# A Mamba-2 block with a routed expert layer: the order of work within a period is moved on all five engines

## The chip, the cores and the metric

The kernel runs on one core of a Trainium2 chip, in one launch. Its time is the device time of that core in microseconds (us). The engines are PE (TensorE matrix products), DVE (VectorE), ACT (ScalarE), POOL (GpSimd) and SP (SyncE, which here only issues transfers). Each engine takes its own list of instructions strictly from front to back; engines wait for each other through semaphores alone.

## The reference

```
x   (16, 512, 128), f32
mod = silu(c) @ wmod                      # sa, ca, ga, sb, cb, gb per sequence
h   = layernorm(x) * (1 + ca) + sa
x   = x + ga * mamba2(h)                  # scan over 512 steps, 4 heads of 64, state 128
h   = layernorm(x) * (1 + cb) + sb
x   = x + gb * moe(h)                     # 8 experts, top 2 of them per token

mamba2: zxbcdt = h @ W_in.T; causal conv of 4 taps and silu over x, B, C
        dt = softplus(dt + dt_bias); state = state * exp(dt*A) + dt*x (outer) B; y = state . C
        y = (y + D*x) * silu(z); y * rsqrt(mean(y*y)+eps) * norm_w; y @ W_out.T
moe:    logits = h @ Wg.T; top 2, softmax of the two
        out = sum over the two experts of w * ((silu(h@W1+b1) * (h@W2+b2)) @ W3 + b3)
```

Everything is f32. The 16 sequences are independent in the Mamba part; the expert part mixes the tokens of all.

## The kernel before, in words

**Pairs.** Two sequences are one pair (8 pairs, 0 to 7). A pair passes these steps, and each is a small function of the kernel: moments1, power_norm1, shift_norm1, normalise1, turn_norm1, modulate1 (first layer norm, transposed into h); project_in 0 to 7 into the two PSUM banks T0 and T1, each followed by conv_first (ACT), conv_taps (DVE) and per channel tile conv_silu (ACT, line 604); project_z and z_silu; time_steps, softplus_exponent, softplus_exp, softplus_rest (dt); masked_da, segments and decay_exp (the decay matrices, through the banks YA and YB); attention, masked_g, mix_chunk; per chunk of 128 steps to_tokens, weight_by_dt and weight_by_decay (POOL, lines 406 and 415), intra, inter, new_state, next_state, y_chunk, turn_y, take_yt, squares; and at the end mean_square, power_y, project_out (line 1389), residual, moments2, power_norm2, shift_norm2, normalise2, turn_norm2, modulate2, logits, turn_h2, load_payload, top_two, which_two, ranks (line 1424), rows, scatter 0 to 7 (POOL, line 427: the pair's rows go to DRAM by expert) and new_tiles, which lists what tiles of one expert's rows are full.

**Tiles.** A tile is 256 rows of one expert; 71 tiles are run, 8 per pair and the last 22 after the last pair. For a tile, SP loads its weights (line 298) and rows (line 318); PE turns the rows (expert_turn, line 1434, bank FX), multiplies them up (expert_up, two halves in banks FG and FV, line 1444) and down (expert_down, lines 1451 and 1457, bank FX again); ACT does expert_input and expert_silu, DVE expert_hidden (line 1125) and expert_out (line 1133); POOL adds the result to the output in DRAM with two indirect DMAs (add_out, line 457). Rows of one token lie in two tiles, so add_out(t) waits until the one before it has landed up to tile 49, and after that only where the two tiles can hold the same token. Tiles 8p-7 to 8p belong to pair p: their rows can be loaded once all eight scatters of pair p have landed. A rows buffer is free again when the add_out seven tiles earlier has landed; a weights buffer after the expert_down four tiles earlier.

**What sets the order.** Each engine has a loop over a period i, whose body is a list of such steps for pairs i-2 to i+3 and tiles 8i-k. The list is fixed text; no scheduler moves anything. While the last steps of pair p run, the first steps of pair p+1 and eight tiles run between them. From pair 3's period on all the tiles of a period are there; before, a period has pair work alone, and after the last pair there are tiles alone.

## Time and profile before

| what | value |
|---|---|
| median of 3 runs | 832.32 us (821.59 to 838.61) |
| profiled execution, its own time | 832.36 us |
| its span | 830.5 us, 1.9 us around it |
| PE / DVE / ACT / POOL busy | 82% / 67% / 62% / 56% of the span |
| mean granted TensorE clock | 0.916 |

The span has four parts. Up to about 246 us there is pair work alone: a period is from one project_out to the next. From there to about 612 us pairs and tiles run together. From 612 us the last pair ends and its rows are scattered, beside tiles of the pair before; from about 709 us only tiles are left. The busy time is an average over these parts, so each is read on its own: from a table of windows, and from the engines' timelines in order of time.

### The profile page before, as it was taken

Reading aid. Unit: us, or ns where it says so; the run is one execution under the profiler, and the core shown is the slowest. Engines: PE = TensorE matmul, PEld = TensorE weight load, DVE = VectorE, ACT = ScalarE, POOL = GpSimd, SP = SyncE. Lnnn points to the kernel's source line nnn. Section 1 sums busy time; section 2 is a strip of 40 time slices with the busy share of each in tenths; the row PEclk is TensorE's granted clock in tenths of the full one; section 3 lists DMA queues with packets and bytes.
Section 4 is the critical chain, followed back from the end, with each engine's and each line's share of the span. In section 5 each row is a group of like instructions: output and inputs, shape, how many; then the busy total and the mean of one; then the engine's idle time right before and its main releaser. Section 6 shows DMA issues by size and latency. Waiting matters only on the chain. (4 is left out here: it accounts for less than half of the span.)

```text
span 830.5 us, 13734 instructions
## 1 busy us (share of the span) xinstructions
PE 680.6 (82%) x3713; PEld 518.9 (62%) x3713; DVE 559.4 (67%) x1640; ACT 516.8 (62%) x1223; POOL 462.0 (56%) x366
## 2 busy tenths in 40 slices
PE   3678899789789999998999999999966952774982
PEld 3246557556567776876787777768755731553662
DVE  2827967988986997898689978987743561231421
ACT  3784795896796899687969977886522310221320
POOL 2003004444453378757775786688687477357775
PEclk9779798999998999999999999999996967897997
DMA  5100001112013465455346444653645774857973
GB/s 186 28 0 1 1 27 32 45 52 71 33 58 102 119 168 129 105 155 125 92 105 174 107 97 103 204 104 90 180 107 120 200 204 95 202 123 149 191 169 28
DMA packets 81275, 88.86 MB, mean 107 GB/s; under 512 B 7360, under 2 KB 67696, under 8 KB 81200
## 3 DMA queue, kind: packets, MB, share of 16 engines
q1 hardware_dynamic: 54528, 61.37, 25.6%
q0 software_dynamic: 26672, 26.62, 18.0%
q8 instruction: 31, 0.51, 0.3%
q14 instruction: 44, 0.36, 0.2%
HBM read 54.50 MB, written 33.46 MB: 106 GB/s over the span
## 5 line engine op out<-in xcount | busy, mean ns | idle before, releaser
L457 POOL DMA_INDIRECT out<-xs x142 | 226.8, 1597 | 116.9 <-issue 53.2
L427 POOL DMA_INDIRECT rows<-payload,pos x128 | 131.6, 1028 | 68.2 <-issue 30.2
L880 DVE SCALAR_TENSOR_TENSOR xbc<-T,table,xbc 128x511 f32<-128x511 f32 (+2 forms) x192 | 141.9, 746 | 7.7 <-ACT xbc L599 3.1
L1133 DVE SCALAR_TENSOR_TENSOR xs<-FX,xs 128x128 f32<-128x128 f32 x142 | 43.1, 345 | 122.6 <-PE FX L1457 104.7
L1457 PE MATMUL FX<-wt,hid 128*128 128x128 f32 x568 | 87.8, 301 | 17.2 <-DVE hid L1125 17.2
L655 ACT ACTIVATE xt<-FX 128x256 f32<-128x256 f32 x71 | 27.0, 380 | 110.1 <-PE FX L1434 96.0
L1457 PEld LDWEIGHTS FX<-wt,hid 128*128 128x128 f32 x568 | 73.7, 203 | 26.6 <-DVE hid L1125 17.9
L648 ACT ACTIVATE sg<-FG,wt 128x256 f32<-128x256 f32 x142 | 59.3, 471 | 47.0 <-PE FG L1444 38.4
L1444 PE MATMUL FG<-xt,wt 128*128 128x256 f32 x284 | 77.6, 397 | 12.1 <-DMA wt<-in_wt 8.1
L1287 PE MATMUL T<-h,win 128*128 128x512 f32 x128 | 76.7, 698 | 12.4 <-DVE xbc L880 10.6
L1444 PE MATMUL FV<-xt,wt 128*128 128x256 f32 x284 | 78.2, 400 | 0.0
L630 ACT ACTIVATE mda<-table,da 128x128 f32<-128x128 f32 x256 | 77.7, 397 | 0.0
L1125 DVE SCALAR_TENSOR_TENSOR hid<-FV,wt,sg 128x256 f32<-128x256 f32 x142 | 62.0, 479 | 22.5 <-issue 13.3
L599 ACT ACTIVATE xbc<-T,table 128x512 f32<-128x512 f32 x64 | 49.5, 773 | 40.3 <-PE T L1287 35.8
L385 POOL TENSOR_TENSOR rstd<-var,table 128x8 f32<-128x8 f32 x16 | 26.6, 1663 | 78.4 <-DVE var L826 63.9
L1346 PEld LDWEIGHTS YA<-xdt,decay 128*128 128x128 f32 x512 | 66.9, 207 | 2.8 <-issue 1.7
L1346 PE MATMUL YA<-xdt,decay 128*128 128x64 f32 x512 | 66.6, 288 | 1.0 <-issue 1.0
L1444 PEld LDWEIGHTS FG<-xt,wt 128*128 128x128 f32 x284 | 52.4, 200 | 20.3 <-DMA wt<-in_wt 9.7
L406 POOL TENSOR_TENSOR xdt<-tok,dt 128x512 f32<-128x512 f32 x32 | 34.8, 1088 | 51.5 <-ACT tok L566 51.3
L527 ACT ACTIVATE xn<-x,shift,rstd 128x128 f32<-128x128 f32 x128 | 50.9, 484 | 17.5 <-DVE shift L844 16.4
L1444 PEld LDWEIGHTS FV<-xt,wt 128*128 128x128 f32 x284 | 52.4, 201 | 8.5 <-issue 3.8
L1434 PE MATMUL FX<-table,xs 128*128 128x128 f32 x142 | 29.3, 290 | 31.8 <-DMA xs<-rows 27.8
(207 smaller groups left out, 1343.5 us busy)
## 6 DMA issues: line engine op xcount, KB each, us to landing
wt<-in_wt SPq DMA_DIRECT2D x71, 386.0 KB
xs<-rows SPq DMA_DIRECT2D x71, 258.0 KB
x<-in_x SPq DMA_DIRECT2D x8, 512.0 KB, 4.3
out<-x SPq DMA_DIRECT2D x8, 512.0 KB
out<-xs POOLq DMA_INDIRECT x142
rows<-pad SPq DMA_DIRECT2D x8, 258.0 KB
rows<-payload,pos POOLq DMA_INDIRECT x128
gate_a<-gates SPq DMA_DIRECT2D x8, 128.0 KB, 4.3
```

The lines of the kernel that those rows point to most:

```text
L427: pool.indirect_dma_start(d["rows"], bass.IndirectOffsetOnAxis(ap=pos[:, k, n:n + 1], axis=0), payload[:, n, :], None).then_inc(scattered, 16)
L457: pool.indirect_dma_start(d["out"], bass.IndirectOffsetOnAxis(ap=xs[:, t % XSR, c, PAY - 1:PAY].bitcast(U32), axis=0), xs[:, t % XSR, c, 0 ...
L527: last = nc.scalar.activation(dst[:, j, :], src[:, j, :], ACT.Identity, bias=shift[:, j:j + 1], scale=rstd[:, j:j + 1])
L599: nc.scalar.activation(xbc[:, t, k, :], T[:, k, :], ACT.Identity, bias=conv_b[:, t:t + 1], scale=conv_w[:, t * KC + KC - 1:t * KC + KC]).t ...
L630: last = nc.scalar.activation(mda[:, c, n, :], upto, ACT.Copy, scale=da[:, c * J + n:c * J + n + 1])
L648: last = nc.scalar.activation(sg[:, t % 2, f * TR:(f + 1) * TR], FG[:, f * TR:(f + 1) * TR], ACT.Silu, bias=wt[:, t % WR, B12 + f:B12 + f ...
L880: last = nc.vector.scalar_tensor_tensor(out=xbc[:, t, k, tap:L], in0=T[:, k, 0:L - tap], scalar=w, in1=xbc[:, t, k, tap:L], op0=ALU.mult, ...
L1125: last = nc.vector.scalar_tensor_tensor(out=hid[:, t % 2, f, :], in0=FV[:, f * TR:(f + 1) * TR], scalar=wt[:, t % WR, B12 + FT + f:B12 + F ...
L1287: nc.tensor.matmul(T[:, k, :], win[:, o:o + P], h[:, k * L:(k + 1) * L], start=True, stop=True).then_inc(in_psum, 1)
L1346: last = nc.tensor.matmul(YA[:, o:o + HD], decay[:, c, k, hh, :], xdt[:, c % 2, k, hh * HD:(hh + 1) * HD], start=True, stop=True)
L1444: last = nc.tensor.matmul((FG, FV)[v][:, f * TR:(f + 1) * TR], wt[:, t % WR, w:w + P], xt[:, t % 2, :], start=True, stop=True)
L1457: last = nc.tensor.matmul(FX[:, TR + c * D:TR + (c + 1) * D], hid[:, t % 2, f, c * P:(c + 1) * P], wt[:, t % WR, DOWN + f * D:DOWN + (f + ...
```

## The change

On every engine the steps of the period are listed in another order. The operations, their sizes, buffers and semaphore waits are the same, and every engine has as many steps as before (PE 660, ACT 557, DVE 420, POOL 223, SP 165). Most of the diff is the same list begun at another step; what is really moved is a few steps against their neighbours. Of each engine the parts that matter, as the diff has them:

```diff
@@ sync
-            for i in range(-1, 13):
...
+            for i in range(1, 14):
+                if is_tile(PT * i - 40):
+                    load_rows(PT * i - 40)
+                if is_tile(PT * i - 39):
+                    load_weights(PT * i - 39)
+                if is_pair(i - 3):
+                    store_x1(i - 3)
+                if is_pair(i):
+                    reload_x(i)
+                if is_tile(PT * i - 39):
+                    load_rows(PT * i - 39)
+                if is_tile(PT * i - 38):
+                    load_rows(PT * i - 38)
+                    load_weights(PT * i - 38)
+                if is_tile(PT * i - 37):
+                    load_weights(PT * i - 37)
+                if is_tile(PT * i - 36):
+                    load_weights(PT * i - 36)
+                if is_tile(PT * i - 37):
+                    load_rows(PT * i - 37)
...
@@ gpsimd
+                if is_tile(PT * i - 27):
+                    add_out(PT * i - 27)
+                if is_pair(i - 2):
                     scatter(i - 2, 7)
+                if is_pair(i):
+                    weight_by_dt(i, 1)
+                    weight_by_decay(i, 1)
                 if is_tile(PT * i - 26):
                     add_out(PT * i - 26)
+                if is_pair(i):
+                    weight_by_dt(i, 2)
                 if is_pair(i + 2):
                     power_norm1(i + 2)
                 if is_pair(i):
-                    weight_by_dt(i, 2)
                     weight_by_decay(i, 2)
                 if is_tile(PT * i - 25):
                     add_out(PT * i - 25)
+                if is_pair(i):
+                    weight_by_dt(i, 3)
                 if is_tile(PT * i - 24):
                     add_out(PT * i - 24)
...
@@ scalar
+                    masked_da(i, 2)
+                    z_silu(i, 3)
+                if is_tile(PT * i - 27):
+                    expert_silu(PT * i - 27)
+                if is_tile(PT * i - 26):
+                    expert_input(PT * i - 26)
+                if is_pair(i + 1):
+                    modulate1(i + 1)
+                if is_pair(i):
+                    conv_silu(i, 3)
                     decay_exp(i, 0)
...
@@ vector
                 if is_pair(i + 1):
                     mix_chunk(i + 1, 1)
+                    mix_chunk(i + 1, 2)
                 if is_pair(i + 2):
                     softplus_exponent(i + 2)
-                if is_pair(i + 1):
-                    y_chunk(i + 1, 0)
-                    next_state(i + 1, 0)
-                    mix_chunk(i + 1, 2)
...
+                if is_pair(i + 2):
+                    softplus_rest(i + 2)
+                if is_tile(PT * i - 13):
+                    expert_hidden(PT * i - 13)
+                if is_tile(PT * i - 14):
+                    expert_out(PT * i - 14)
+                if is_pair(i + 2):
+                    conv_taps(i + 2, 4)
+                    conv_taps(i + 2, 5)
...
@@ tensor
                 if is_pair(i):
-                    turn_y(i, 1)
-                if is_tile(PT * i - 21):
-                    expert_turn(PT * i - 21)
+                    turn_y(i, 0)
+                if is_tile(PT * i - 24):
+                    expert_down(PT * i - 24)
+                if is_pair(i):
+                    new_state(i, 2)
+                    intra(i, 1)
+                if is_pair(i - 1):
+                    turn_h2(i - 1)
```

ACT, end of a period with no tile yet (pair 3's steps; mda is masked_da, zs is z_silu, xbc is conv_silu 3, h is modulate1, decay is decay_exp), before:

```order
L630 ACTIVATE mda<-table,da 128x128 x8
L611 ACTIVATE zs<-YB 128x512
L604 ACTIVATE xbc<-xbc 128x1024
L534 ACTIVATE h<-T,mod 128x512 x2
L623 ACT_TABLE_LOAD
```

and now:

```order
L633 ACTIVATE mda<-table,da 128x128 x8
L614 ACTIVATE zs<-YB 128x512
L537 ACTIVATE h<-T,mod 128x512 x2
L607 ACTIVATE xbc<-xbc 128x1024
L626 ACT_TABLE_LOAD
```

modulate1 stands ahead of conv_silu 3. The number of table loads on ACT is 28 in both.

PE, a period with tiles, up to ranks (S<-table,y is turn_y 0; YA is intra 1; T<-table,h is turn_h2; FX<-b_parts and FX<-wt are expert_down; S<-xdecay is new_state 2; FG is the first half of expert_up; S<-hots begins ranks), before:

```order
L1377 MATMUL S<-table,y 128x128 x4
L1346 MATMUL YA<-xdt,decay 128x64 x8
L1434 MATMUL FX<-table,xs 128x128 x2
L1408 MATMUL T<-table,h 128x128 x8
L1451 MATMUL FX<-b_parts,sel 128x256
L1457 MATMUL FX<-wt,hid 128x128 x4
L1366 MATMUL S<-xdecay,tok 128x256 x2
L1444 MATMUL FG<-xt,wt 128x256 x2
L1424 MATMUL S<-hots,ones_r 128x64
```

and now:

```order
L1440 MATMUL FX<-table,xs 128x128 x2
L1422 MATMUL S<-table,h 128x8 x8
L1362 MATMUL YB<-state,xbc 128x256 x2
L1383 MATMUL S<-table,y 128x128 x4
L1457 MATMUL FX<-b_parts,sel 128x256
L1463 MATMUL FX<-wt,hid 128x128 x4
L1372 MATMUL S<-xdecay,tok 128x256 x2
L1352 MATMUL YA<-xdt,decay 128x64 x8
L1414 MATMUL T<-table,h 128x128 x8
L1450 MATMUL FG<-xt,wt 128x256 x2
L1440 MATMUL FX<-table,xs 128x128 x2
L1430 MATMUL S<-hots,ones_r 128x64
```

The bank S is filled by new_state 2 earlier, with intra 1 and turn_h2 between it and ranks; the expert_turn that stood behind intra 1 is now ahead of logits (S<-table,h) and inter 1 (YB).

DVE, the end of softplus_rest (L873, now L877) in the same period, before:

```order
L873 TENSOR_TENSOR da<-dt,nega 128x32
L1133 SCALAR_TENSOR_TENSOR xs<-FX,xs 128x128 x2
L880 SCALAR_TENSOR_TENSOR xbc<-T,table,xbc 128x511
L880 SCALAR_TENSOR_TENSOR xbc<-T,table,xbc 128x510
L880 SCALAR_TENSOR_TENSOR xbc<-T,table,xbc 128x509
L1125 SCALAR_TENSOR_TENSOR hid<-FV,wt,sg 128x256 x2
```

and now:

```order
L877 TENSOR_TENSOR da<-dt,nega 128x32
L1129 SCALAR_TENSOR_TENSOR hid<-FV,wt,sg 128x256 x2
L1137 SCALAR_TENSOR_TENSOR xs<-FX,xs 128x128 x2
L884 SCALAR_TENSOR_TENSOR xbc<-T,table,xbc 128x511
L884 SCALAR_TENSOR_TENSOR xbc<-T,table,xbc 128x510
```

The next tile's expert_hidden (hid) stands right behind softplus_rest, ahead of three conv taps.

## Rows read from the trace of the kernel before

**Rows 1.** Windows: length, busy us of PE, PEld, DVE, ACT, POOL; clock, DMA share, GB/s
```profile
181.60:246.10 64.50, 52.51 (x294) 38.45 (x295) 57.63 (x170) 52.54 (x125) 29.00 (x28) 0.97 0.16 54
...
319.30:399.40 80.10, 76.94 (x446) 60.40 (x446) 66.91 (x198) 63.67 (x150) 56.29 (x45) 0.96 0.51 123
399.40:475.20 75.80, 73.86 (x447) 58.65 (x447) 66.00 (x195) 63.55 (x151) 53.78 (x42) 1.00 0.53 130
475.20:549.70 74.50, 72.79 (x439) 57.79 (x440) 62.66 (x175) 59.03 (x140) 52.90 (x43) 1.00 0.51 125
549.70:612.20 62.50, 58.94 (x384) 48.58 (x383) 43.66 (x135) 38.62 (x97) 48.59 (x37) 1.00 0.57 138
```

**Rows 2.** Timeline of POOL, 640 to 662 us: start, duration, instruction, idle before
```profile
648.43 1.55 POOL L457 DMA_INDIRECT out<-xs  x1 [4.88 <-DMA out<-xs]
```

**Rows 3.** Timeline of ACT, 238.5 to 248 us, same columns
```profile
243.63 1.06 ACT L604 ACTIVATE xbc<-xbc 128x1024 f32<-128x1024 f32 x1
244.58 1.45 ACT L534 ACTIVATE h<-T,mod 128x512 f32<-128x512 f32 x2
```

**Rows 4.** Timeline of PE, 239.5 to 250 us
```profile
242.62 1.06 PE L1265 MATMUL T<-table,xn 128*128 128x128 f32 x8 [0.44 <-DVE xbc L880]
...
246.13 3.81 PE L1389 MATMUL T<-wo,yt 128*128 128x128 f32 x32 [1.13 <-ACT h L534]
```

**Rows 5.** Timeline of DVE, 197 to 201 us
```profile
198.41 0.69 DVE L933 TENSOR_TENSOR ysum<-YA,xskip 128x512 f32<-128x512 f32 x1 [0.65 <-PE YA L1346]
```

**Rows 6.** Timelines of POOL and of PE, 77 to 90 us (pair 0)
```profile
79.77 1.64 POOL L385 TENSOR_TENSOR rstd<-var,table 128x8 f32<-128x8 f32 x1 [8.90 <-PE YA L1346]
...
83.63 2.05 PE L1366 MATMUL S<-xdecay,tok 128*128 128x256 f32 x4 [3.90 <-issue]
```

**Rows 7.** Timeline of PE, 430 to 442.3 us
```profile
433.25 1.90 PE L1346 MATMUL YA<-xdt,decay 128*128 128x64 f32 x16
434.99 0.39 PE L1434 MATMUL FX<-table,xs 128*128 128x128 f32 x2
435.21 1.04 PE L1408 MATMUL T<-table,h 128*128 128x128 f32 x8
436.18 0.28 PE L1451 MATMUL FX<-b_parts,sel 32*128 32x256 bf16 x1
...
437.38 1.03 PE L1366 MATMUL S<-xdecay,tok 128*128 128x256 f32 x4
438.25 1.03 PE L1444 MATMUL FG<-xt,wt 128*128 128x256 f32 x4
440.17 1.05 PE L1424 MATMUL S<-hots,ones_r 128*128 128x64 f32 x8 [0.89 <-DVE state L920]
```

**Rows 8.** Timeline of PE, 456 to 471 us (project_z 3)
```profile
468.43 1.10 PE L1299 MATMUL YB<-win,h 128*128 128x256 f32 x4 [0.78 <-ACT zs L611]
```

**Rows 9.** Timeline of DVE, 453.6 to 466 us
```profile
457.17 0.60 DVE L1133 SCALAR_TENSOR_TENSOR xs<-FX,xs 128x128 f32<-128x128 f32 x2
...
459.91 0.86 DVE L1125 SCALAR_TENSOR_TENSOR hid<-FV,wt,sg 128x256 f32<-128x256 f32 x2
```

**Rows 10.** Timeline of PE, 381.5 to 392 us
```profile
385.30 0.28 PE L1451 MATMUL FX<-b_parts,sel 32*128 32x256 bf16 x1 [2.23 <-ACT xt L655]
```

**Rows 11.** Table of windows, the five microseconds behind that wait
```profile
385.00:390.00 5.00, 4.70 (x16) 3.32 (x17) 2.35 (x6) 4.91 (x13) 3.80 (x4) 0.66 0.57 100
```

**Rows 12.** Timeline of POOL, 574 to 604 us
```profile
590.18 1.55 POOL L457 DMA_INDIRECT out<-xs  x1 [4.48 <-DMA out<-xs]
...
596.54 1.05 POOL L406 TENSOR_TENSOR xdt<-tok,dt 128x512 f32<-128x512 f32 x1
```

**Rows 13.** Timeline of POOL, 752 to 775 us
```profile
766.90 1.55 POOL L457 DMA_INDIRECT out<-xs  x1 [1.14 <-DVE xs L1133]
```

**Rows 14.** Timelines of POOL and of SP, 412 to 431 us (scatter 7, rows of the next tile)
```profile
422.25 1.39 POOL L427 DMA_INDIRECT rows<-payload,pos  x1 [0.30 <-issue]
...
426.00 0.37 SPq L318 DMA_DIRECT2D xs<-rows  x1
```

More of the change, by code:

```diff
@@ L695, in _ @@
                     expert_input(PT * i - 24)
+                if is_tile(PT * i - 25):
+                    expert_silu(PT * i - 25)
                 if is_pair(i):
@@ new lines, in _ @@
+                if is_pair(i + 2):
+                    conv_taps(i + 2, 0)
+                if is_pair(i):
+                    take_logits(i)
+                if is_pair(i + 2):
+                    conv_taps(i + 2, 1)
+                if is_pair(i):
+                    top_two(i)
+                    which_two(i)
+                if is_pair(i + 1):
+                    next_state(i + 1, 2)
+                if is_tile(PT * i - 16):
+                    expert_out(PT * i - 16)
+                if is_pair(i + 1):
+                    y_chunk(i + 1, 1)
@@ new lines, in _ @@
+                if is_pair(i):
+                    rows(i)
+                if is_tile(PT * i - 15):
+                    expert_hidden(PT * i - 15)
+                if 0 < i + 3 < NP:
+                    shift_norm1(i + 3)
+                if is_pair(i + 2):
+                    conv_taps(i + 2, 2)
+                if is_pair(i + 1):
+                    y_chunk(i + 1, 2)
+                if is_tile(PT * i - 15):
+                    expert_out(PT * i - 15)
+                if is_pair(i + 2):
+                    conv_taps(i + 2, 3)
```

447 lines of the change are left out of this document (187 added, 260 removed).

## The prediction

> **What bounds the kernel now.** I read the table of windows first, cut at the starts of project_out, because the page's 82% for PE is an average over parts with different limits. The reader is to see four of them [rows 1]. (a) A period of pair work alone, 64.50 us: PE works 52.51, DVE 57.63, ACT 52.54; nobody is full, and the length comes out of a ring of waits that crosses the engines. (b) The periods with tiles, 80.10, 75.80 and 74.50 us: PE works 76.94, 73.86 and 72.79 of them, so PE is the bound and only what lies in its few idle microseconds can be won; DVE, at 66 of 75.8, is close behind. (c) The last pair's period of 62.50 us, and (d) everything behind it. For (d) I read POOL's timeline: an add_out waits until the one before has landed, and it issues 4.88 us after its predecessor's last DMA [rows 2]. Two DMAs of about 1.6 us, 0.3 between them, and this wait are some 8.3 us per tile, whatever PE does, and from add_out 32, at 590.18 [rows 12], up to tile 49 the tiles follow each other so, with scatters in some of the pauses. The end of the kernel is therefore the moment at which POOL enters that chain plus a near-constant 240 us. An edit pays if it brings (a) or (b) to an end earlier, or takes POOL work out of the chain.
>
> **The change, part by part.** The sum is made against the profiled execution, 832.36 us (span 830.5 and 1.9 around it), which is the median of the runs, 832.32, to within 0.1.
>
> *modulate1 ahead of conv_silu 3.* In a pair-only period conv_silu 3 starts at 243.63 and modulate1 only at 244.58 [rows 3], while turn_norm1, its input, is done at 242.62 + 1.06 = 243.68; project_out then waits 1.13 us for it [rows 4] and the residual, the moments and the next period hang on project_out. Moved ahead, modulate1 starts at about 243.7: 0.9 us. The decay exponents behind both come at the same time as now.
>
> *y_chunk 0 behind all four mix_chunks.* DVE idles 0.65 us before it for intra 0 [rows 5]; the later place fills that with work it has to do anyway. DVE is then without a pause up to the convolution taps of the next pair, which set turn_norm1 [rows 4], so the 0.65 arrives there too. Both together: 0.9 + 0.65, taken as 1.5 us per pair-only period, as turn_norm1 and modulate1 then end up within 0.1 us of each other. Ends: 0 (another of the ring's waits takes over) and 2.6 (all of the 1.13 and 0.44 and more that these two engines idle there). There are two such periods at full effect (115 to 246 us): -3.0. In the third (246 to 319 us), which gets its first tiles halfway, I take 1.0: -1.0.
>
> *Pair 0.* weight_by_dt 2 goes ahead of power_norm1, which took 1.64 us [rows 6] while weight_by_dt could already have run; new_state 2, which waits for the decayed copy, can start 1.0 us (one weight_by_dt) sooner. But intra 1 (433.25 to 434.99, 1.74 us at full clock [rows 7]) now stands behind new_state 2 and ahead of project_in 2, where it used to fill part of the 3.90 us idle [rows 6]: +1.7. With modulate1's -0.9 this is -0.2; I count 0. Ends -1 and +2.
>
> *The periods with tiles.* Two waits of PE go. ranks waits 0.89 us for next_state 2 to free the bank S [rows 7]; intra 1 and turn_h2, 1.74 + 0.97 us, now lie between, and next_state 2 stands ahead of expert_out: gone. project_z 3 waits 0.78 us for a z_silu [rows 8]; three blocks of PE now lie in front of it instead of one: gone. -1.67 per period.
> Two come. First, expert_hidden for the next tile stands behind softplus_rest and PE's second expert_up of the tile after needs it. From the start of ranks, PE now comes to that expert_up after 13 blocks of 0.87 us (437.38 to 438.25 [rows 7]), intra 2 with 1.74, two expert_downs of 1.20 (436.18 to 437.38), two turns of 0.22, a turn_y of 0.4 and ranks itself with 1.1, together 17.4 us. DVE's list up to the end of softplus_rest is today's, which ends 17.0 us after ranks starts (457.17 less 440.17 [rows 9, 7]), plus the expert_out of 0.60 that now comes behind next_state 2, plus the expert_hidden of 0.86: 18.5. So PE waits about 1.0 us with project_in and project_z queued behind. Second, logits and turn_y 0 share S with next_state 1 and take_logits; expert_up is no longer between them. Adding the blocks in the same way, turn_y comes 0.5 us too early and the expert_turn in front of logits 0.4. +1.9. The net is +0.2, in four periods +1. Ends: -1.67 each, -7, if the new waits don't arise; +1.9 each, +8, if the old ones only move.
> At waits of this size one more thing has to be judged: the clock. A wait of 2.23 us [rows 10] was followed by a granted clock of 0.66 over five microseconds [rows 11], that is, part of it at 1.2 GHz, and its period is the 80.10 one, 5.6 more than the shortest [rows 1]. Periods with waits of 0.89 and 0.78 kept 1.00 in every one of their windows [rows 1]. So waits of about a microsecond cost themselves and no more, and the sum has nothing for the clock. The Trainium skill says otherwise in one place: "TensorE: Matmul & The Clock Gate", A second HAM failure mode: psum-queue depth-cycling, tells of a kernel whose brief idles between groups of products, from cycling through PSUM banks, were enough to make the clock swing between its two levels. By that rule the new waits would cost the price of the slow rival below, and not +1.
>
> *scatter 7 ahead of weight_by_dt 1, and the expert_turn that needs it ahead of logits.* Rows of the next pair's first tile are loaded 2.4 us after the last scatter, whose second DMA is at 422.25 to 423.64 [rows 14]; PE used them at 434.99 [rows 7], so the landing after 426.00 took 9 us at most; I take 4. scatter 7 is now one weight_by_dt and one weight_by_decay (1.04 each) and their pause earlier, about 3 us: rows there at 427. The turn's new place is at about 429. Cover 2 us, cost nothing; if it is gone, PE stands with logits and all of the routing behind it, 1 us a period if the scatter comes as late as today. weight_by_decay 1 comes 3 us later, at 422, against a use at 425: covered as well.
>
> *POOL in the last pair.* weight_by_dt 3 now stands between add_out 31 and 32, where POOL idled 4.48 us for the landing, and no longer between two scatters, where it cost 1.05 in a stretch without a pause [rows 12]: -1.2 with its gap. What could take it away is intra 1 of the last pair, which it waits for and which ends near 583 now, 1.7 later then, against 586. Ends 0 and -1.2.
>
> *SP.* Three weight loads of a period now go ahead of three row loads that wait for landings. In the last part, a weight load stuck behind such rows made tile 57 late, and its add_out waited 1.14 us for expert_out [rows 13]: -1.1. In return three row loads stand behind the weights of a tile whose expert_down has to be done; behind them PE might wait 2 to 3 us at tiles 51, 59 and 67, in a part where POOL's chain sets the time: 0. Ends -2 and +3. Within the pair periods weights are issued several tiles ahead: 0.
>
> Sum: 832.4 - 3.0 - 1.0 + 0 + 1 - 1.2 - 1.1 = **827**.
>
> **The rivals.**
> *Faster.* The 80.10 us period falls to its neighbours' 74.5 as its 2.23 us wait is not met again (-5.6), the old waits go and no new ones come (4 times -1.67, -6.7), the pair-only periods give 2.0 each (-4), and POOL and SP -2.3 with 1 for the third period: 832.4 - 19.6 = 813. For it: the wait of 2.23 was on expert_input, which no step of that place made late. Against it: DVE's list is nearly full too. 0.17.
> *Slower.* The wait behind softplus_rest grows. It is 1.0 us by my count, and everything that delays DVE in the eight steps ahead of it adds to it; if it reaches about 2 us the clock falls as it did at 385 us, and a period costs 5.6 more [rows 1, 10, 11]. In all four periods with tiles: 827 + 22.4 = 849, with the third period as well 855; I take 852. It decides at a wait of 2 us: below, it adds its length alone, up to 4 more in all. For it: PE is full, so nothing is given back. Against it: the products behind project_out's wait of 1.13 us ran at full speed, 3.81 for the 32 of them [rows 4]. 0.13.
> *No gain.* What the pair periods win is met by POOL's chain, which keeps its own pace from the first tiles of the last pairs on, or by waits elsewhere in the ring: 832.4 - 1.2 = 831. POOL idles for PE's results in the periods with tiles, which speaks against it. 0.2.
> *The loads.* The rows behind scatter 7 come too late for the earlier turn, 1 us in each of four periods, and the first wait of new order another 1: 827 + 8 = 835. 0.08.
>
> My forecast keeps 0.42. Forecast, no gain and the loads lie within 2% (815.7 to 849.0), about what a measurement of this kernel can tell from no change; the slow rival begins at that edge, so its 0.13 is slower by over 2%, and 0.02 of the loads' as well. The fast rival is over 2%, with 0.01 for a still better ring. That makes 0.18 faster, 0.67 same, 0.15 slower. The range goes from 814 to 843: it holds the forecast, no gain and the loads with the bounds of the unknown costs (-7 and +8 in the tiled periods, -1 and +2 in pair 0), and leaves the larger part of the two outer cases out.
>
> **What would show it.** Periods from project_out to project_out of about 63 us in the pair-only part, with project_out's wait for modulate1 near 0.1 to 0.4; no wait of ranks for next_state, one of about 1 us on the second expert_up behind softplus_rest; a clock of 1.00 in the tiled periods; POOL's idle before add_out 32 near 3.4 instead of 4.48; add_out 57 without its wait. Tiled periods of 75 to 76 us say that the trade was even; 80 with a clock below 1.00 is the slow rival; 73 the fast one. Wrong would be the whole reading if the time from add_out 32 to the end were other than 240 us by more than 5.

## The result: 0.9% slower

| | before | changed |
|---|---|---|
| median | 828.58 us (20 runs, 819.56 to 838.61, and one of 1119.24 among them) | 831.96 us (20 runs, 828.98 to 839.88) |
| profiled execution | 832.36, span 830.5 | 839.43, span 837.5 |
| project_out 7 starts at | 612.24 | 628.35 |
| from there to the end | 218.3 | 209.2 |

The ratio of changed to before is 1.0094, 95% interval 1.0062 to 1.0125, where 827 against 832.4 (0.9935) was forecast: clear of noise, and under 2%. The 832.4 that the forecast starts from is a single profiled execution, 3.8 us above the median of these 20. The changed kernel's profiled execution is one of its longest; a second one, of 830.5, stands beside it below where that matters.

The table of windows of the changed kernel, cut as in [rows 1]; the first two are the pair-only periods.

```profile
core 0: us, PE busy (x) PEld busy (x) DVE busy (x) ACT busy (x) POOL busy (x), PEclk, DMA share, GB/s
114.90:185.70 70.80, 62.41 (x294) 47.05 (x295) 56.51 (x160) 52.25 (x125) 25.81 (x23) 0.81 0.12 40
185.70:253.30 67.60, 58.01 (x295) 43.48 (x295) 57.89 (x167) 52.44 (x125) 30.55 (x28) 0.87 0.19 59
253.30:328.50 75.20, 71.86 (x407) 56.38 (x408) 64.57 (x180) 61.66 (x146) 44.14 (x35) 0.95 0.47 124
328.50:409.80 81.30, 78.50 (x448) 62.02 (x447) 69.50 (x197) 63.48 (x151) 57.31 (x46) 0.94 0.52 124
409.80:487.60 77.80, 75.66 (x447) 59.55 (x446) 68.90 (x194) 63.10 (x151) 53.92 (x42) 0.98 0.51 124
487.60:562.50 74.90, 73.26 (x440) 57.95 (x440) 64.13 (x179) 60.63 (x142) 54.33 (x43) 1.00 0.53 125
562.50:628.40 65.90, 60.67 (x384) 50.25 (x383) 43.31 (x139) 38.23 (x98) 50.38 (x40) 0.97 0.53 125
```

Read it in three quantities. **Idle** is length less PE busy: in the second period 67.60 - 58.01 = 9.6, against 12.0 before. The waits of PE did get fewer. **Busy** rose in that period from 52.51 to 58.01 with the same 295 products: the same work was done at a lower clock. The lower of the clock's two levels (1.2 of 2.4 GHz) is 0.5 in this column, so (1 - clock) x 2 x length is the time spent at it, which I call low clock below: 2 x 0.13 x 67.6 = 18 us against 4, and 27 against 11 in the period before it. **DVE busy** rose from 66.0 to 68.9 in the period 409.8 to 487.6 and by half of that in the next one (62.7 to 64.1), with the same operations. The last two are the losses; the gain is behind 628.

What the prediction said would show: project_out's wait for modulate1 went, from 1.13 [rows 4] to 0.19. PE, changed kernel (start, duration, instruction, idle before):

```profile
253.29 2.92 PE L1395 MATMUL T<-wo,yt 128*128 128x128 f32 x24 [0.19 <-ACT h L537]
```

ranks no longer waits in the periods with tiles, and nothing waits at expert_up behind softplus_rest. Instead, expert_turn waits ahead of logits, in its new place:

```profile
440.87 0.41 PE L1440 MATMUL FX<-table,xs 128*128 128x128 f32 x2 [1.20 <-DVE xs L1137]
441.11 1.85 PE L1422 MATMUL S<-table,h 128*128 128x8 f32 x16
```

It waits for DVE's expert_out, which frees the bank FX. DVE was late because of one instruction, the last of moments1. DVE and POOL of the changed kernel, side by side:

```profile
436.41 0.17 DVE L829 TENSOR_SCALAR within<-within 128x8 f32<-128x8 f32 x1
436.61 2.27 DVE L830 TENSOR_TENSOR var<-within,apart 128x8 f32<-128x8 f32 x1
438.80 0.68 DVE L918 TENSOR_TENSOR faded<-state,edge 128x512 f32<-128x512 f32 x1
...
436.15 1.61 POOL L459 DMA_INDIRECT out<-xs  x1 [0.30 <-issue]
437.19 1.65 POOL L408 TENSOR_TENSOR xdt<-tok,dt 128x512 f32<-128x512 f32 x1
438.96 2.06 POOL L387 TENSOR_TENSOR rstd<-var,table 128x8 f32<-128x8 f32 x1
```

The same instruction before, and POOL beside it:

```profile
429.10 0.17 DVE L826 TENSOR_TENSOR var<-within,apart 128x8 f32<-128x8 f32 x1
...
429.36 1.67 POOL L385 TENSOR_TENSOR rstd<-var,table 128x8 f32<-128x8 f32 x1 [1.56 <-DVE var L826]
431.01 1.03 POOL L406 TENSOR_TENSOR xdt<-tok,dt 128x512 f32<-128x512 f32 x1
```

Eight columns take 2.27 us and end where POOL's weight_by_dt 2 ends; I call this the lock below. Before, POOL stood idle for `var` at that moment, since power_norm1 was first in its list; the change put weight_by_dt 2, which needs no `var`, ahead of it. This happens in the periods from 328 and from 410, and not from 488, where no pair is left for moments1, and DVE's busy time is nearer to what it was.

### The profile page after: what moved, and what is told of

It is laid out like the page before. It is cut to its first block and busy times, and to the rows that moved or that the text cites. A ratio compares the mean times of both kernels' runs of the same rounds, so it can differ in the third digit from the quotient of the medians.

```text
span 837.5 us, 13738 instructions
## 1 busy us (share of the span) xinstructions
PE 706.0 (84%) x3713; PEld 538.7 (64%) x3713; DVE 567.7 (68%) x1640; ACT 515.4 (62%) x1223; POOL 471.5 (56%) x366
## 5 line engine op out<-in xcount | busy, mean ns | idle before, releaser
L1463 PE MATMUL FX<-wt,hid 128*128 128x128 f32 x568 | 90.3, 307 | 0.5 <-DVE hid L1129 0.5
L1293 PE MATMUL T<-h,win 128*128 128x512 f32 x128 | 80.9, 744 | 11.5 <-DVE xbc L884 8.3
L408 POOL TENSOR_TENSOR xdt<-tok,dt 128x512 f32<-128x512 f32 x32 | 38.8, 1212 | 85.3 <-ACT tok L569 44.5
L1450 PE MATMUL FV<-xt,wt 128*128 128x256 f32 x284 | 80.5, 409 | 5.6 <-DVE hid L1129 5.0
L1450 PE MATMUL FG<-xt,wt 128*128 128x256 f32 x284 | 80.8, 411 | 2.5 <-DMA wt<-in_wt 1.1
L1463 PEld LDWEIGHTS FX<-wt,hid 128*128 128x128 f32 x568 | 75.7, 207 | 10.1 <-issue 2.2
L1352 PEld LDWEIGHTS YA<-xdt,decay 128*128 128x128 f32 x512 | 73.7, 225 | 10.4 <-ACT zs L614 6.3
L1352 PE MATMUL YA<-xdt,decay 128*128 128x64 f32 x512 | 73.7, 307 | 6.5 <-ACT zs L614 4.6
L387 POOL TENSOR_TENSOR rstd<-var,table 128x8 f32<-128x8 f32 x16 | 28.9, 1808 | 64.7 <-DVE var L830 59.1
L1450 PEld LDWEIGHTS FG<-xt,wt 128*128 128x128 f32 x284 | 54.6, 210 | 11.1 <-issue 4.2
```

Source lines behind the costliest of these rows:

```text
L1293: nc.tensor.matmul(T[:, k, :], win[:, o:o + P], h[:, k * L:(k + 1) * L], start=True, stop=True).then_inc(in_psum, 1)
L1352: last = nc.tensor.matmul(YA[:, o:o + HD], decay[:, c, k, hh, :], xdt[:, c % 2, k, hh * HD:(hh + 1) * HD], start=True, stop=True)
L1450: last = nc.tensor.matmul((FG, FV)[v][:, f * TR:(f + 1) * TR], wt[:, t % WR, w:w + P], xt[:, t % 2, :], start=True, stop=True)
L1463: last = nc.tensor.matmul(FX[:, TR + c * D:TR + (c + 1) * D], hid[:, t % 2, f, c * P:(c + 1) * P], wt[:, t % WR, DOWN + f * D:DOWN + (f + ...
```

## The experiments

Ratios are to the kernel before, run on the same chip, with their 95% intervals. "Old" is an order as before, "new" as changed. P1 and P2 are the two pair-only periods, P3 the third, P4 to P6 the full ones with tiles, P7 the last pair's.

### Is it the clock or the waits?

The changed kernel as it is, a second time: 1.0074 (1.0050 to 1.0099).

> The changed kernel once more, unaltered, for a second profile and more times. Its profiled execution of 839.43 us had PE's clock at its lower level (1.2 GHz) for about 27 us of the period 115 to 186 and for 18 us of the one after it, where the kernel before had 11 and 4. Theory (the clock, not the waits, lengthens the pair-only periods): the executions differ among themselves by how long the clock is low, so an execution near 831 us has at least 8 us less of low clock in the pair-only part than the profiled one, and its periods are shorter by about half of that; PE's idle time in them stays at 8 to 10 us. Rival (the new waits are what lengthens the periods): an execution that is shorter has less idle time of PE in them, at the same clock.

Both changed and before with idle time filled:

```diff
+            def filler(when, n):
+                if when:
+                    for _ in range(n):
+                        nc.tensor.matmul(FG[:, 0:256], ident, win[:, 0:256], start=True, stop=True)
...
                 if is_pair(i):
+                    filler(i in (1, 2), 4)
                     intra(i, 3)
```

> The changed kernel with products that nobody reads (256 columns, 0.43 us each at the full clock, into the bank FG, which no tile uses yet) ahead of six waits of PE in each of the two pair-only periods (115 to 253 us). They are sized to lie inside the idle times (intra 3 1.9 to 2.8, ranks 1.9, project_in 5 1.3, turn_norm2 0.95, project_in 0 and new_state 2 0.7). Clock theory: the clock stays at 1.00 there or nearly so (under 10 us of low clock in both periods together, against 44), each period falls from 70.8 and 67.6 to about 63 to 65, project_out 2 comes about 8 us sooner, and the whole is about 5 us faster, since the tail hides a part. Wait theory: the low clock isn't what costs, the periods stay at 68 to 71 or grow by what the fillers overrun.

> The kernel before with such products ahead of seven waits of PE in the two pair-only periods. Its profiled execution had 14.5 us of low clock there. Clock theory: that goes to under 5, the two periods (66.4 and 64.5) come to about 63 each, 3 to 5 us in all, and the kernel is 2 to 4 us faster than before. Wait theory: nothing, or slower by the fillers that overrun.

The execution of 830.5 had P1 and P2 of 69.1 and 67.6 us with 21 and 18 us of low clock: not shorter by less idle time (9.5 and 9.6), as the clock theory said, though by 6 us of low clock rather than 8. But fillers brought 1.0064 (1.0044 to 1.0084) and 0.9985 (0.9964 to 1.0005), too little to tell from no effect. In the changed kernel they did raise the clock (low clock in P1 and P2 7 and 7 us instead of 21 and 18), and P1 fell to 65.6, but P2 stayed at 67.2. In the old one low clock went from 11 to 0 in P1 and from 4 to 7 in P2, and P2 came to 67.0. That the fillers' own 6 to 7 us a period pushed the ring is my reading, not shown. Low clock costs, as the executions below show, and wasn't bought off this way.

The next pair put two such products ahead of attention, where PE waits for nothing, and ahead of the place where the clock fell in P2 and P3 of each changed profile:

```diff
                 if is_pair(i + 1):
+                    filler(i in (0, 1, 2), 2)
                     attention(i + 1)
```

> The changed kernel with two products of 256 columns that nobody reads (0.86 us together) ahead of attention in the two pair-only periods and in the third. PE waits for nothing there; behind it stand products of 128, 4 and 64 columns, and in all three profiles of the changed order the clock falls to its lower level about 13 us after project_out, at intra 0 (6.8 us of low clock at 198 to 206 and again at 266 to 274). Theory A (the clock falls there for what PE does and not for a wait, and the period pays half of it): those two stretches go or halve, the third period falls from 74.8 to 72 or less, the second from 67.6 to about 66, and the kernel is 2 to 4 us faster than the changed one. Theory B (these products only cost their time, or the low stretch comes anyway): the same lows, each period 0 to 0.9 us longer.

> The kernel before with SP's new list and the same two products ahead of attention. SP's list alone gave 821.98 against 826.96. In its profile 6.8 us of low clock came at 195 to 203, at intra 0, in others of the old order there was none in the second or third period. Theory A: 1 to 2 us faster than with SP's list alone, as this stretch then never comes. Theory B: the same or up to 2.5 us slower (three times 0.86).

1.0056 (1.0023 to 1.0090) and 0.9955 (0.9928 to 0.9982), against 1.0074 and 0.9946 without these products: nothing gained. In the changed kernel's P2 the fall at intra 0 (198 us in the execution of 830.5) was gone, but low clock came at 213 to 221 instead, and P3's stayed. Where in the period the clock falls I can't steer, and why it does stays open.

What can be read is its price. Of P2 there are many executions with the same, or nearly the same, lists on PE, ACT and DVE. Old order, low clock 4 us: 64.5; 14 us: 67.3 to 68.5; 17 us: 69.0, here beside P5 (the kernel with SP's new list):

```profile
181.80:250.80 69.00, 58.57 (x294) 43.92 (x295) 57.34 (x173) 52.54 (x125) 28.91 (x28) 0.88 0.19 62
...
397.10:472.90 75.80, 73.84 (x447) 58.59 (x447) 66.21 (x196) 63.44 (x151) 55.68 (x44) 1.00 0.54 130
```

That is (69.0 - 64.5) / 13 = 0.35 us per us of low clock. New order, 13 us: 66.2; 18 us: 67.6, six times. At an equal clock the new ring is 1 to 2 us shorter than the old; but in the new order P1 and P2 had 13 to 27 us of low clock in every profile without fillers, in the old 4 to 17. In whole runs it is the same: mean granted clock 0.906 in 26 runs of the changed kernel, 0.921 in 115 of before.

### The two swaps of the pair-only term, alone

```diff
+                if is_pair(i + 2):
+                    modulate1(i + 2)
                 if is_pair(i + 1):
                     conv_silu(i + 1, 3)
-                if is_pair(i + 2):
-                    modulate1(i + 2)
...
-                    y_chunk(i + 1, 0)
                     next_state(i + 1, 0)
...
                     mix_chunk(i + 1, 3)
+                    y_chunk(i + 1, 0)
```

> The kernel before with only two moves of the change: on ACT modulate1 ahead of conv_silu 3, on DVE y_chunk 0 behind all four mix_chunks. The prediction counted -1.5 us for each pair-only period and -1.0 for the third, 4 us in all. Theory A (these terms are right, and something else in the change costs): at the same amount of low clock the two pair-only periods are 1 to 2 us shorter than before's 66.4 and 64.5 (which had 10.6 and 3.9 us of low clock), the wait of project_out for modulate1 (1.13) is under 0.5, and the kernel is 2 to 4 us faster. Theory B (another wait of the ring takes their place): the periods stay within 0.5 us at the same clock, the kernel within 1 us.

1.0041 (1.0012 to 1.0069), slower. The window of P2 and two lines of PE:

```profile
183.70:248.50 64.80, 52.51 (x294) 38.60 (x295) 56.73 (x170) 52.30 (x125) 28.59 (x28) 0.97 0.16 54
```

```profile
212.62 0.66 PE L1377 MATMUL S<-table,y 128*128 128x128 f32 x4 [2.22 <-DVE logit L974]
...
248.51 3.70 PE L1389 MATMUL T<-wo,yt 128*128 128x128 f32 x31 [0.28 <-ACT h L534]
```

The wait for modulate1 is gone (0.28), and turn_y 0 waits 2.22 us instead of 1.09. It doesn't wait for y_chunk 0, which is done at 206.5, but for what the line names: take_logits, which frees the bank S at 212.56. DVE reaches take_logits 0.9 us later after project_out than before (28.63 us instead of 27.72), and its timeline shows where that comes from:

```profile
194.91 0.85 DVE L895 COPY fade<-decay 128x32 f32<-128x32 f32 x1 [1.97 <-ACT decay L623]
...
202.19 0.69 DVE L910 COPY state<-S 128x512 f32<-128x512 f32 x1 [2.17 <-PE S L1366]
...
205.78 0.69 DVE L935 TENSOR_TENSOR y<-ysum,zs 128x512 f32<-128x512 f32 x1
...
212.35 0.21 DVE L974 COPY logit<-S 128x64 f32<-128x64 f32 x1
```

Before, `fade` waited 0.98 for the decay exponents, and next_state 0 (L910) nothing:

```profile
192.08 0.20 DVE L895 COPY fade<-decay 128x32 f32<-128x32 f32 x1 [0.98 <-ACT decay L623]
...
200.53 0.68 DVE L910 COPY state<-S 128x512 f32<-128x512 f32 x1
```

So neither gain got through. project_out starts 0.85 us sooner, but ACT's decay exponents don't, and DVE waits 1 us more for them. And y_chunk 0 had stood where DVE has to wait for new_state 0 anyway; with it moved, DVE is idle there for 2.17 us instead of 0.65 ahead of y_chunk 0, and does y_chunk 0 (1.4) later on top. At the same clock, 0.97, P2 is 64.8 against 64.5. The term is 0, not -1.5. Pair 0's period was 118.9 here; in the other profiles of the kernel before and of its variants it was 113.4 to 117.0. One thing differs from the full change: there mix_chunk 2 stands ahead of next_state 0 as well. Its next_state 0 waits all the same, 2.42 us in P2:

```profile
207.32 0.69 DVE L914 COPY state<-S 128x512 f32<-128x512 f32 x1 [2.42 <-PE S L1372]
```

modulate1's swap alone, on top of SP's new list:

> The kernel before with SP's new list and, on ACT, modulate1 ahead of conv_silu 3. With both swaps the wait of project_out was gone, but turn_y 0 waited 2.2 us instead of 1.1 for y_chunk 0, and pair 0's period was 3.5 us longer. Here y_chunk 0 stays. If modulate1's 0.9 us is real: pair-only periods 0.5 to 1 us shorter at the same amount of low clock, and 1 to 2 us faster than SP's list alone (0.9946). If the ring has another wait ready: no difference.

0.9903 (0.9869 to 0.9938), the fastest kernel here, ahead of both given ones. Against SP's list alone (below) the intervals overlap, and its P1, at the same low clock of 11 us, is 66.5 against 66.4, with `fade` waiting 1.97 for the decay exponents instead of 1.23. That modulate1 adds anything is not shown.

### Whose list costs?

SP's list exchanged alone, in the kernel before and, the other way round, in the changed one:

```diff
@@ sync
-            for i in range(-1, 13):
...
+            for i in range(1, 14):
...
```

> The kernel before with the changed kernel's SP order alone. The prediction counted -1.1 us for it (add_out 57 without its wait of 1.14) and nothing else. After the last project_out the changed kernel needs 209.2 us against 218.3. Theory A (SP's order gives that back): this kernel is 2 us or more faster than before, its add_outs between tile 48 and 70 closer. Theory B (only the later start of the tail, with more rows ready, makes it shorter): this kernel is within 1 us of before apart from the -1.1.

> The changed kernel with SP's list as it was before. The reverse exchange gave 0.9946 (about 4.5 us faster with the new SP list). Theory A (SP's order gains that by itself, whatever the rest): this kernel is 3 to 6 us slower than the changed one, 834 to 837, with the time from add_out 32 to the end 1 to 2 us longer. Theory B (the gain depends on the other orders): within 2 us of the changed kernel's 830.8.

0.9946 (0.9915 to 0.9976), and 1.0412 (1.0383 to 1.0441). SP's new order gains 0.5% in the old kernel, and without it the new one loses 3%: its P3 to P5 are 79.0, 85.4 and 82.1. The gain in the old kernel is in the tail. POOL's add_out 57, with the old list (the two swaps) and with the new (the changed kernel):

```profile
763.84 1.55 POOL L457 DMA_INDIRECT out<-xs  x1 [4.02 <-DMA out<-xs]
```

```profile
773.03 1.55 POOL L459 DMA_INDIRECT out<-xs  x1 [0.30 <-DMA out<-xs]
```

In four profiles with SP's old list, from add_out 56 to 57 it took 4.59, 6.47, 6.71 and 7.47 us, and from add_out 38 to the end 187.1 to 191.4; with the new list 3.7 to 4.5, and 183.3 to 187.1 in sixteen. The profile I predicted from had the smallest of the four. With the old list the weights of tile 58 are issued behind three loads of rows, and PE, which has the first half of tile 58's expert_up ahead of tile 57's expert_down, waits for them (the two swaps):

```profile
758.00 2.07 PE L1444 MATMUL FG<-xt,wt 128*128 128x256 f32 x4 [6.39 <-DMA wt<-in_wt]
760.00 0.39 PE L1451 MATMUL FX<-b_parts,sel 32*128 32x256 bf16 x1
```

On the mean of the profiles, add_out 38 to the end is 190.0 with the old list and 184.8 with the new, and add_out 56 to 57 gives 2.5 of these 5.1 us. Another 3.0 lie between add_outs 38 and 44 (49.9 against 46.9), and no run isolates why.

Then POOL's list, and POOL's and ACT's, on top of SP's (`@@ gpsimd`, `@@ scalar` exchanged in the same way), and in the changed kernel DVE's taken back (`@@ vector`):

> The kernel before with SP's and POOL's new lists, PE, ACT and DVE as before. The prediction gave POOL -1.2 us (weight_by_dt 3 between add_out 31 and 32) and called the earlier scatter 7 covered. SP's list alone gave 0.9946. If POOL's term is right: 0.9930 or so, add_out 32 about 1 us earlier than in the kernel with SP's list alone (585.4). If POOL's new order only fits the new PE order: 0.995 or above.

> SP's, POOL's and ACT's new lists, PE and DVE as before. Theory A (PE's and DVE's new lists are what costs, by their waits and by the clock): this kernel stays near the one without ACT's list, within 1 us, and nearly all of the distance to the changed kernel (1.007 to 1.009) lies in PE and DVE. Theory B (ACT's list costs, as modulate1 ahead of conv_silu 3 holds back to_tokens): 2 us or more slower than without it.

> The changed kernel with DVE's list as it was before (y_chunk 0 ahead of mix_chunk 2, expert_hidden not behind softplus_rest). The prediction blamed DVE's new order for the wait of about 1 us on expert_up and gave it the gain of 0.65 in the pair-only periods. Theory A (DVE's order is what costs in the tiled periods): the waits of 1.2 and 1.4 us ahead of expert_turn go, periods 402 to 480 at about 75.8, 2 us or more faster than the changed kernel. Theory B (PE's and DVE's lists belong together): PE waits more, 3 us or more slower.

1.0036 (0.9998 to 1.0075), 1.0642 (1.0585 to 1.0698) and 1.1005 (1.0956 to 1.1053). POOL's list costs 0.9% on top of SP's, ACT's another 6% until PE's and DVE's come with it, and the new PE list with the old DVE list has P4 to P6 of 95 us. The lists are one schedule; a list's worth can't be added up from exchanges, only single steps can be judged.

### The single steps of the tiled periods

PE's expert_turn back behind turn_y 0:

```diff
@@ tensor
                     turn_y(i, 0)
+                if is_tile(PT * i - 23):
+                    expert_turn(PT * i - 23)
...
-                if is_tile(PT * i - 15):
-                    expert_turn(PT * i - 15)
```

> The changed kernel with one step of PE moved back: the expert_turn that stood ahead of logits stands behind turn_y 0 again, as before. In the changed kernel it waits 1.15 to 1.20 us for expert_out of the tile two before (bank FX) with logits queued behind, and low clock follows 2 us later (3.4 to 6.8 us of it at 358 to 368, once also at 443). Theory A (this wait is what lengthens the tiled periods): the wait goes, the periods 325 to 402 and 402 to 480 fall from 76.8 and 77.6 to about 75.8 as before, no low clock near 358; 2 to 3 us faster than the changed kernel. Theory B (the wait moves to the next instruction that needs DVE, since DVE's list is late): PE's idle time in these periods stays at 1.5 to 3.1, no faster.

1.0140 (1.0105 to 1.0174), slower still. The wait of 1.20 is gone, waits of 0.68, 0.68 and 0.47 have come elsewhere in P5, and P4 and P5 are 78.6 with 6.3 us of low clock each (the second execution of the changed kernel: 76.8 and 77.6). The wait is not what lengthens these periods by itself.

POOL's weight_by_dt 2 back behind power_norm1, and, from the other side, DVE's moments1 back behind next_state 1:

```diff
@@ gpsimd
-                if is_pair(i):
-                    weight_by_dt(i, 2)
                 if is_pair(i + 2):
                     power_norm1(i + 2)
                 if is_pair(i):
+                    weight_by_dt(i, 2)
                     weight_by_decay(i, 2)
```

```diff
@@ vector
-                if 0 < i + 3 < NP:
-                    moments1(i + 3)
                 if is_pair(i + 1):
                     next_state(i + 1, 1)
                 if is_tile(PT * i - 17):
                     expert_out(PT * i - 17)
+                if 0 < i + 3 < NP:
+                    moments1(i + 3)
```

> The changed kernel with one POOL step moved back: weight_by_dt 2 stands behind power_norm1 again. In the changed kernel the last instruction of moments1 on DVE, 128x8 elements from two tensors in SBUF, takes 2.23 to 2.27 us in the periods 325 to 402 and 402 to 480 and 0.17 everywhere before the change; it ends just as POOL's weight_by_dt 2 does. Theory A (DVE and POOL shut each other out, and these 2.1 us of DVE are what lengthens the tiled periods): the instruction is back at 0.17, the two periods fall from 76.8 and 77.6 by 1 to 1.9 us to about 75.8, the waits of expert_turn (1.2 and 1.4) shrink, and the kernel is 2 to 4 us faster than the changed one (ratio to before about 1.004). Theory B (the order of PE against DVE costs, the lock is hidden): the instruction is short again but the periods stay within 0.5 us.

> The changed kernel with one DVE step moved back: moments1 stands behind next_state 1, as before, and also behind expert_out. Theory A (the lock): var is written while POOL is at other work or not, the long instruction goes or another one meets POOL in its place; with expert_out 2.5 us earlier the wait of 1.2 us of expert_turn ahead of logits goes in any case. 2 to 4 us faster than the changed kernel. Theory B: the clock eats what the waits gave, as in the kernel with expert_turn moved back: waits gone, low clock 6.3 us a period, no faster.

> The changed kernel with both: weight_by_dt 2 behind power_norm1 and the expert_turn behind turn_y 0, as before. If the lock costs about 2 us and the turn's wait 1.2 in each of two periods and they are the same microseconds seen from two engines, this is as fast as with weight_by_dt 2 alone; if they add, the periods are at 75.5 or less and the kernel 1 to 2 us faster than that.

The one POOL step gives 0.9984 (0.9950 to 1.0018): the changed kernel's whole loss against the kernel before, though not the gain of SP's list. Its windows P4 and P5, then DVE and POOL:

```profile
325.00:400.00 75.00, 74.10 (x448) 58.55 (x447) 66.83 (x196) 63.52 (x151) 56.30 (x44) 1.00 0.54 131
400.00:475.10 75.10, 74.19 (x448) 58.61 (x447) 66.97 (x196) 63.57 (x151) 56.31 (x44) 1.00 0.54 131
```

```profile
426.81 0.17 DVE L829 TENSOR_TENSOR var<-within,apart 128x8 f32<-128x8 f32 x1
426.89 0.69 DVE L917 TENSOR_TENSOR faded<-state,edge 128x512 f32<-128x512 f32 x1
...
427.39 2.28 POOL L387 TENSOR_TENSOR rstd<-var,table 128x8 f32<-128x8 f32 x1
429.10 1.59 POOL L408 TENSOR_TENSOR xdt<-tok,dt 128x512 f32<-128x512 f32 x1
```

`var` takes 0.17 again, DVE is busy 67.0 instead of 69 to 69.8, PE idles 0.9, and the periods are 75.0 and 75.1, against 76.8 and 77.6 with the stretched instruction. Was it the add_out beside which `var` runs, and not weight_by_dt 2? No: here too `var` lies inside an indirect DMA of add_out, and is short; only what POOL does next is another:

```profile
426.36 1.61 POOL L459 DMA_INDIRECT out<-xs  x1 [0.30 <-issue]
```

Of the 6.7 us between this profile (span 821.8) and the changed kernel's second one (828.5), 4.4 lie in P4 and P5 and 2.2 in P7, where the clock was low for 4 us instead of 11. P4's 1.8 are in good part clock too (3 us low, against none), P5's 2.6 are nearly all idle time of PE (3.1 against 0.9).

With moments1 moved instead, `var` is short too, but the kernel is at 1.0082 (1.0053 to 1.0111): P4 and P5 are 78.6, again with 6.3 us of low clock, which at half of it (PE is the bound here) leaves 75.4, an estimate. So the lock's cost is shown from POOL's side, and from DVE's only after taking off the clock. With both steps back it is 1.0146 (1.0101 to 1.0191), P5 79.1: moving the turn costs with or without the lock.

The same POOL step, the first of these two diffs read backwards, made in the old kernel with SP's new list; and POOL's whole old list in the changed kernel:

> The kernel before with SP's new list (0.9946 by itself) and the one POOL step that cost the changed kernel 1%: weight_by_dt 2 ahead of power_norm1. If the lock between DVE and POOL does it whatever the other lists are: 1.5 us or more slower than with SP's list alone, and an instruction of DVE near moments1 stretched by about 0.6 to 2 us in the periods 322 to 473, which go from 75.8 to 77 or more. If it needs DVE's new place for moments1: within 1 us of SP's list alone, nothing stretched.

> The changed kernel with POOL's whole list as before; with weight_by_dt 2 alone moved back it came to 0.9984. If the rest of POOL's new order (scatter 7 ahead of weight_by_dt 1, weight_by_dt 3 between add_outs) gains as the prediction said, this is 1 us or more slower than 0.9984 gave; if it costs in the pair-only periods too (POOL stretched there by 2.1 to 2.6 us a period against 0.1 to 0.9 before), they get shorter than 68.8 and 67.6 and this is faster. If PE's new order needs it, a wait of PE for rows or xdt shows and it is 3 us or more slower.

The first is 0.9969 (0.9937 to 1.0002), not told apart from 0.9946, and its P4 and P5 are 74.9, shorter than 75.8. DVE and POOL show why it costs nothing there:

```profile
419.41 1.64 DVE L822 BATCH_NORM_STATS2 stats<-x 128x6 f32<-128x128 f32 x8
421.08 0.47 DVE L824 TENSOR_TENSOR mv<-stats 128x8 f32<-128x8 f32 x1
...
419.85 1.66 POOL L408 TENSOR_TENSOR xdt<-tok,dt 128x512 f32<-128x512 f32 x1
422.28 1.67 POOL L387 TENSOR_TENSOR rstd<-var,table 128x8 f32<-128x8 f32 x1 [0.77 <-DVE var L829]
```

Here weight_by_dt 2 runs beside the statistics, which read one tensor, and they keep their pace (1.64 for eight); only `mv`, 0.47 instead of 0.17, meets its end. In the old kernel the step costs nothing; to stretch `var` it needs DVE's new place for moments1 as well. The second is 1.0034 (1.0004 to 1.0063). Its P4 and P5:

```profile
324.50:398.50 74.00, 73.63 (x448) 58.55 (x447) 67.64 (x196) 63.36 (x151) 56.10 (x43) 1.00 0.57 133
398.50:472.60 74.10, 73.84 (x448) 58.54 (x447) 67.99 (x196) 63.36 (x151) 56.04 (x44) 1.00 0.57 133
```

74.0: the old waits gone and next to no new ones, and 1.7 less than before, as the prediction's -1.67 has it. It loses that again in P3 (75.4, with 11 us of low clock), the last pair (P7 67.8) and the tail (238.0 from add_out 32 on).

## Why the prediction was wrong, step by step

- **Pair-only periods, -3.0 and -1.0: wrong.** Two steps failed. "DVE is then without a pause up to the convolution taps of the next pair": it isn't. y_chunk 0 had filled most of DVE's wait for new_state 0, and without it next_state 0 waits 2.17 us (two swaps) and 2.42 (changed kernel, P2). And modulate1's 0.9 was carried past project_out without asking what else DVE needs there: the decay exponents, which I had said "come at the same time as now", and for which DVE then waits 1 us more. The change's other edits shortened the ring all the same, by 1 to 2 us at equal clock. The low clock took that back and more in P1 (21 and 27 us of it in the changed kernel's two executions, 69.1 and 70.8 us long, against 4 to 11 and 64.6 to 67.3 in the old order); P2's 67.6 lies within the old order's 64.5 to 69.0. P3 had 7 us of low clock or more in every changed profile and none in six of eight old ones: 74.8 and 75.2 in the changed kernel's two executions against 70.5 to 71.3 in those six.
- **"The sum has nothing for the clock": wrong.** I had kept it for waits of 2 us, since P5 kept 1.00 with waits of 0.89 and 0.78. The same profile had the counterexample: in P4 the same wait of 0.89 ends at 360.05, and low clock follows there as well, not only at 385:

```profile
360.05 1.05 PE L1424 MATMUL S<-hots,ones_r 128*128 128x64 f32 x8 [0.89 <-DVE state L920]
```

The window from 362.5 to 366 us, columns as in the table at the top, has a clock of 0.52:

```profile
362.50:366.00 3.50, 3.50 (x9) 1.59 (x8) 3.11 (x12) 2.11 (x4) 1.18 (x2) 0.52 0.97 261
```

In the changed kernel the wait of 1.20 at 440 was followed by 3.4 us of low clock at 443 in one execution and by none in the other, and in the profiled one, four of the nine falls from P1 to P6 had no wait of PE over 0.8 us in the five us ahead. What makes the clock fall stays open. The 80.10 of P4 that I took as a base was one execution's: seven other profiles of the old order have 74.9 to 79.1 there. The rule I weighed and set aside, in the Trainium skill's "TensorE: Matmul & The Clock Gate", A second HAM failure mode: psum-queue depth-cycling, is nearer to these traces than my row: short idles, a clock swinging between both levels. Its cause, though, isn't shown here: filling the idles did not pay.
- **Periods with tiles, +0.2 each: mechanism half right, size wrong.** Gone are 0.89 and 0.78, as said. The wait I charged at 1.0 behind softplus_rest never came; DVE was held up earlier, by 2.1 us of a blocked instruction in P4 and P5, and PE paid 1.20 ahead of logits and up to 1.42 at the next expert_turn. P4 and P5 came to 76.8 and 77.6 in the execution of 830.5, +1.0 and +1.8. I had listed weight_by_dt 2 ahead of power_norm1 for pair 0 alone, as a gain of 1.0, and never laid POOL's timeline over DVE's. Of all the steps taken back, this is the one that brings the kernel to 0.9984, level with before.
- **scatter 7 and the earlier turn: cover enough.** The turn waited for the bank and not for its rows; the loads rival is out.
- **POOL in the last pair, -1.2: not to be read off.** weight_by_dt 3 does fill the pause ahead of add_out 32, but after a wait of 1.77 for intra 1, the thing I named as able to spoil it; POOL idles 2.99 there in two pieces instead of 4.48:

```profile
599.44 1.04 POOL L408 TENSOR_TENSOR xdt<-tok,dt 128x512 f32<-128x512 f32 x1 [1.77 <-PE YA L1352]
601.70 1.93 POOL L459 DMA_INDIRECT out<-xs  x1 [1.22 <-DMA out<-xs]
```

- **SP's order, -1.1: right sign, a quarter of the size.** About 5 us of the tail, the largest single gain of the change, and half of it at the place I named. One profile's wait of 1.14 was an easy case of a wait that was 1.14 to 4.02 in the four profiles; the other half, ahead of add_out 44, I hadn't foreseen.
- **The end as add_out 32 plus 240: not to the 5 us I had set.** It was 240.3 before and 235.8 in the changed kernel's profiled execution, but 234.5 in its second one; over all profiles 236.2 to 241.0 with SP's old list and 232.2 to 238.0 with the new. It is near enough constant that add_out 32, at 601.7 and 594.0 instead of 590.2, is where the losses ahead arrive.
- **The slow rival** had the right kind of cost, a fall of the clock, but the wrong place and condition (waits of 2 us behind softplus_rest); P3, where it came, paid 4.3. The lock between DVE and POOL was in none of the cases.
- **The no-gain rival's 831** is nearest to the 832.0 measured, by luck: it starts from 832.4, and against the median of 828.6 the kernel lost 3.4 us.

The account, in the execution of 830.5 against the kernel with SP's new list alone (822.1): add_out 32 at 594.0 against 585.4, and the same 234.5 and 234.9 behind it. Of the 8.6, P3 gave 4.3 (nearly all clock), P4 and P5 2.9, P1 and P2 1.3, and the way from project_out 6 to add_out 32 1.4; the pair 0 part took 1.4 back.

## What to carry to other kernels

When an instruction of POOL is moved, lay its new place over DVE's timeline and look at what two-tensor instructions of DVE run there; a wait that POOL had may have been what kept it off DVE. When a step is made later, look at the wait that it was filling: the instruction behind it may then stand idle for as long as the step took. When a step comes sooner, list everything that its successors wait for; the gain goes no further than the latest of it. And take a wait's size from several executions if it depends on which of two queues is ahead: one profile gave 1.1 for what can be 4.

## What the runs showed of the hardware

- DVE's `var`, 128x8 from two tensors in SBUF, took 0.17 us alone and 2.27 beside POOL's weight_by_dt 2; the statistics, with one input, took 1.64 for eight beside the same instruction and without it. The Trainium skill, "SBUF — State Buffer", section "SBUF: two separate sides", says that a DVE operation with two SBUF inputs and a GpSimd operation that reads SBUF exclude each other for a whole instruction; the trace agrees that they do, and that an instruction with one input is spared. Which of the two gets hold first isn't shown here: by the records `var` began 0.58 us ahead of weight_by_dt 2 and was held even so, and POOL's spans are rough.
- Two executions with the same lists on PE, DVE, ACT and POOL differed by 4.5 us in P2, 64.5 and 69.0, with 4 and 17 us of low clock; PE's idle time was shorter in the longer one (10.4 against 12.0). In P2 of the changed kernel's two executions the falls came at the same places, to 0.2 us from project_out 1:

```profile
196.00:200.00 4.00, 3.74 (x33) 3.50 (x32) 2.99 (x4) 3.74 (x13) 3.65 (x4) 1.00 0.00 0
200.00:208.00 8.00, 8.00 (x40) 7.42 (x40) 5.54 (x8) 2.75 (x6) 6.43 (x5) 0.57 0.37 115
208.00:224.00 16.00, 11.71 (x77) 9.35 (x76) 14.84 (x59) 9.93 (x23) 4.21 (x3) 1.00 0.01 2
224.00:228.00 4.00, 4.00 (x14) 2.66 (x13) 3.76 (x14) 1.81 (x2) 0.00 (x0) 0.58 0.58 143
```

Ahead of 200 PE was busy 3.74 of 4.00 us, with products of 4 and 128 columns; through 208 to 224 it idled 4.3 of 16 and kept 1.00. In these stretches PE's busy share does not tell where the clock falls.
